# A windowed strain attention with a top-4 of 16 expert layer: the experts' work by dispatch in groups, four strains of eight on TensorE, the damage bias inside its product

## The reference

```
disp = (x @ W_disp)            # 16 heads of 16
strain = disp_win - disp       # 64 earlier positions of each token
bond_act = gelu(strain @ W_strain + rel_emb @ W_pos)
damage_act = gelu(strain @ W_dmg + b_dmg)
damage = sigmoid(damage_act @ W_dmg_out + b_dmg_out)
logits = bond_act @ W_bond - 10.0 * damage
out = softmax(logits) @ val_win @ W_cproj
```

```
vals, idx = top_k(t @ gate_w.T + gate_b, 4); w = softmax(vals)   # 4 of 16 experts per token
h = t @ w1[e] + b1[e];  s = swiglu(h);  y = s @ w2[e] + b2[e]
acc = acc + route[e] * y       # the reference does it for all 16 experts
```

## Time and profile before

| | us |
|---|---|
| median of three runs (range) | 1205.12 (1204.17 to 1207.86) |
| span of the profiled execution | 1203.6 |
| the profiled execution's own time stands among the three runs; its span is below it by | 0.6 to 4.3 |
| set-up block | 0 to 41.1 |
| loop 1, band 1 | 41.1 to 327.5, to 406.0 |
| loop 2, band 2 | 406.0 to 692.5, to 772.0 |
| second layer | 772.0 to 1203.6 |
| busy in the span: PE, DVE, ACT, POOL | 1056.1, 962.4, 821.7, 168.1 |

### The profile page before, as it was taken

One profiled execution on the slowest core, in us unless ns is written; L12 is line 12 of the kernel. 1 busy time (PEld: TensorE's weight loads), 2 busy tenths in 40 slices (PEclk: granted clock), 3 DMA queues, 4 the chain that ended last, 5 costly groups with the idle time before them and its releaser, 6 DMA issues. The chain is left out here.

```text
span 1203.6 us, 23755 instructions
## 1 busy us (share of the span) xinstructions
PE 1056.1 (88%) x9995; PEld 567.0 (47%) x9995; DVE 962.4 (80%) x1193; ACT 821.7 (68%) x888; POOL 168.1 (14%) x265
## 2 busy tenths in 40 slices
PE   6499888998879499889899868999999999999897
PEld 4233333333368333333333368853654565655533
DVE  7899999999763799999999863557778577676757
ACT  3689999999763489999989862243156666665464
POOL 5100000000140100000000050232760000000072
PEclk9699999999979789999999979999779999999899
DMA  8400000000075200000000057000132344523121
GB/s 269 128 2 2 1 1 2 1 1 2 1 204 145 54 1 2 1 1 2 1 1 2 1 172 178 24 1 1 36 105 62 105 132 125 155 80 90 47 60 45
DMA packets 71754, 67.45 MB, mean 56 GB/s; under 512 B 6148, under 2 KB 63200, under 8 KB 71648
## 3 DMA queue, kind: packets, MB, share of 16 engines
q1 hardware_dynamic: 66264, 55.31, 16.1%
q0 software_dynamic: 3840, 10.43, 3.3%
q10 hardware_dynamic: 1544, 0.20, 0.1%
HBM read 41.80 MB, written 20.97 MB: 52 GB/s over the span
## 5 line engine op out<-in xcount | busy, mean ns | idle before, releaser
L580 DVE SCALAR_TENSOR_TENSOR ring<-AD,PT 128x1808 f32<-128x1808 f32 (+15 forms) x128 | 286.1, 2235 | 3.8 <-POOLq L562 1.9
L725 PE MATMUL LG<-ring,lred 128*32 128x456 f32 (+15 forms) x2048 | 233.4, 575 | 2.0 <-ACT ring L677 2.0
L1932 DVE TENSOR_REDUCE MX<-SS 128x2 f32<-128x1024 f32 x119 | 144.6, 1219 | 55.3 <-PE SS L1649 55.2
L1862 ACT ACTIVATE EX<-SS 128x1024 f32<-128x1024 f32 x128 | 130.4, 1031 | 80.4 <-PE SS L1649 79.8
L667 ACT ACTIVATE ring<-ring 128x3616 f32<-128x3616 f32 (+15 forms) x50 | 169.9, 3398 | 3.7 <-DVE ring L580 3.7
L747 PE MATMUL SD<-DS,eyes 96*32 96x456 bf16 (+15 forms) x2496 | 156.2, 369 | 10.1 <-ACT ring L672 8.1
L675 ACT ACTIVATE ring<-ring 128x1824 f32<-128x1824 f32 (+15 forms) x78 | 141.0, 1808 | 0.0
L747 PEld LDWEIGHTS SD<-DS,eyes 96*32 96x32 bf16 x2496 | 58.0, 96 | 154.6 <-ACT ring L672 56.7
L580 DVE SCALAR_TENSOR_TENSOR ring<-AD,bdmg 128x1808 f32<-128x1808 f32 (+15 forms) x50 | 111.4, 2228 | 0.0
L725 PEld LDWEIGHTS LG<-ring,lred 128*32 128x32 f32 x2048 | 59.4, 110 | 100.2 <-issue 76.6
L760 PE MATMUL PY<-w2T,xg 128*128 128x128 f32 x512 | 75.6, 292 | 31.5 <-DVE xg L605 31.5
(11 more groups left out here) (346 smaller groups left out, 1558.0 us busy)
## 6 DMA issues: line engine op xcount, KB each, us to landing
w1s<-in_L_ffn_W SPq DMA_DIRECT2D x39, 256.0 KB, 3.0
w2s<-in_L_ffn_W SPq DMA_DIRECT2D x39, 256.0 KB, 2.9
band<-zs SPq DMA_DIRECT2D x8, 1024.0 KB, 9.9
wide<-band POOLq DMA_DIRECT2D x16, 380.0 KB, 8.3
wide<-band SPq DMA_DIRECT2D x16, 380.0 KB, 10.0
band<-Z SPq DMA_DIRECT2D x4, 1024.0 KB, 7.7
xs<-Z SPq DMA_DIRECT2D x4, 640.0 KB, 8.0
xl<-xs SPq DMA_DIRECT2D x10, 256.0 KB, 2.9
```

The source lines that it names most:

```text
L580: return v.scalar_tensor_tensor(out=ring[:, slot, s, :, t0:T], in0=AD[:, s, :, j + t0:j + T], scalar=extra, in1=AD[:, s, :, PAD + t0:PAD + T],
L725: mm = pe.matmul(LG[32 * b:32 * b + 32, par, s, t0:T], lred[:, s, n % 4, :], ring[:, slot, s, b, t0:T], start=(n % 4 == 0), stop=(n % 4 == 3))
L1862: act.activation(EX[:, Q % 2, hh:hh + 2, t, :], SS[:, slot, :, :], ACT.Exp, scale=SCALE1).then_inc(freed[slot], 1)
L1932: v.tensor_reduce(MX[:, t, p // 2, hh:hh + 2], pairs_of(b, name), AX.X, ALU.max).then_inc(freed[slot], 1)
```

## The change

**Experts by dispatch.** Each token's four slots in a buffer sorted by expert, in tiles of 128 rows, are computed in the first body of loop 1 (`count`, `starts`, `tables` on TensorE, `expert_tiles`, `token_slots`, `tile_tables` on VectorE). POOL scatters the normalised rows into DRAM (`xs0`) with 64 indirect transfers. 80 tiles, in 20 groups of four (A and B of a body), go through bodies 4 to 7 of loop 1 and 0 to 5 of loop 2 (MOE_ITS). For a group, SP loads the rows (`tokens`, one buffer `xl`), four first weights (`weights1`, two buffers) and four second weights (`weights2`, one buffer), each weight's address from a table value that it loads first, and stores the result (`store`). TensorE turns the rows (`turn`), and then the steps are as before, in four pieces of 128 where the expert differs; `move_out` copies the result out. In the end POOL gathers each token's four rows (64 indirect transfers: 32 in loop 2 after the last group, 32 in band 2), and VectorE adds them with `add_rows`.

**Strains.** PE_ITEMS becomes (1, 3, 5, 7), in the first body (3, 5, 7): VectorE makes four damage strains of eight (before, three), TensorE four (before, five), in alternation.

**Bias.** The product takes 99 rows in place of 96: the three parts of `b_dmg` against rows of ones in `DS`, which POOL writes once per loop (3 rows of 9216); the Gelu needs no bias operand.

**Zeroing.** The clearing of `band` and of the second layer's `xs` goes from the set-up block into loop 1 on SP; `xs0` is cleared in the set-up block, and both weight stacks are written to DRAM there.

The core of the diff:

```diff
-PE_ITEMS = (1, 2, 4, 6, 7)
-AFTER_PE = (2, 7)
-FIRST_PE_ITEMS = (2, 4, 6, 7)
+PE_ITEMS = (1, 3, 5, 7)
+FIRST_PE_ITEMS = (3, 5, 7)
 NPE = len(PE_ITEMS)
 LOOP_PE = 7 * NPE + len(FIRST_PE_ITEMS)
...
+MOE_ITS = ((4, 5, 6, 7), (0, 1, 2, 3, 4, 5))
...
+    def gather(pool, k, half, dst):
+
+        for t in range(8 * half, 8 * half + 8):
+            pool.indirect_dma_start(dst[:, t, :], None, ys0[:, :], bass.IndirectOffsetOnAxis(ap=sloti[:, t, k:k + 1], axis=0),
+                                    bounds_check=ROWS0 - 1, oob_is_err=True).then_inc(d_yg[half] if k < 3 else d_yh, 16)
...
+                def tokens(n):
+                    sp.wait_ge(tok_turned, n)
+                    sp.dma_start(xl[:], xs0[4 * P * n:4 * P * n + 4 * P, :].rearrange("(n p) c -> p n c", p=P)).then_inc(d_xl, 16)
+
+                def weights1(n):
+                    if n >= 2:
+                        sp.wait_ge(h_ready, n - 1)
+                    for a in range(4):
+                        e = sp.value_load(owneri[0:1, 4 * n + a:4 * n + a + 1], min_val=0, max_val=E0 - 1)
+                        sp.dma_start(w1s[:, n % 2, a, :], w1d[bass.ds(e, 1), :, :].rearrange("o p i -> p (o i)")).then_inc(d_w1[n % 2], 16)
+
+                def weights2(n):
+                    if n:
+                        sp.wait_ge(y_ready, n)
+                    for a in range(4):
+                        e = sp.value_load(owneri[0:1, 4 * n + a:4 * n + a + 1], min_val=0, max_val=E0 - 1)
+                        sp.dma_start(w2s[:, a, :], w2d[bass.ds(e, 1), :, :].rearrange("o p c -> p (o c)")).then_inc(d_w2, 16)
+
+                def store(n):
+                    sp.wait_ge(y_used, n + 1)
+                    sp.dma_start(ys0[4 * P * n:4 * P * n + 4 * P, :].rearrange("(n p) c -> p n c", p=P), yo[:]).then_inc(d_ys, 16)
...
+                    sp.wait_ge(d_small, 96)
+                    sp.wait_ge(small_pool, 6)
+                weights1(groups[0])
+                weights2(groups[0])
+                if g == 0:
+                    sp.wait_ge(d_scatter, 16 * TT * K0)
+                tokens(groups[0])
+                for n in groups:
+                    if n + 1 in groups:
+                        weights1(n + 1)
+                        tokens(n + 1)
+                        weights2(n + 1)
+                    store(n)
+                sp.wait_ge(d_ys, 16 * (groups[-1] + 1))
...
+                    for t in range(TT):
+                        for k in range(K0):
+                            pool.indirect_dma_start(xs0[:, :], bass.IndirectOffsetOnAxis(ap=sloti[:, t, k:k + 1], axis=0), TF[:, t, :], None,
+                                                    bounds_check=ROWS0 - 1, oob_is_err=True).then_inc(d_scatter, 16)
+                else:
+                    pool.wait_ge(d_ys, 16 * GROUPS0)
+                    for k in range(2):
+                        for half in range(2):
+                            if k:
+                                pool.wait_ge(added, 2 * k + half - 1)
+                            gather(pool, k, half, yg0)
...
+                    A, B_ = moe_groups(g, it)
+                    before = moe_groups(g, it - 1)[1] if it else None
+                    item(4, it)
+                    item(5, it)
+                    move_out(before)
                     if it:
                         logits(1, 2 * it - 1)
...
+                    item(6, it)
+                    glu_in(A)
...
+                    item(7, it)
+                    move_in(B_)
+                    item(8, it)
+                    glu_out(A)
                     logits(0, 2 * it)
-                    glu_out(3, u + 3)
-                    combine(2, it, u + 2)
...
+                        tile_tables()
...
+                    item(9, it)
...
+                        add_rows(v, 0, 1, yg0)
+                    item(10, it)
+                    move_out(A)
+                    item(11, it)
+                    glu_out(B_)
+                    if (g, it) == (1, 7):
+                        add_rows(v, 1, 0, yg0)
...
-                            for q in range(4):
-                                mm = pe.matmul(SD[32 * q:32 * q + 32, i, t0:T], eyes[0:96, sign, :], DS[0:96, q, 2 * half + i, at:at + T - t0],
-                                               start=(sign == 0), stop=(sign == 1))
+                    for i in range(2):
+                        for q in range(4):
+                            pe.matmul(SD[32 * q:32 * q + 32, i, t0:T], eyes[0:99, q, :], DS[0:99, q, 2 * half + i, j + t0:j + T],
...
+                def turn(n):
+                    if n is not None:
+                        pe.wait_ge(d_xl, 16 * (n + 1))
+                        pe.wait_ge(xg_ready, n)
+                        for a in range(4):
+                            mm = pe.transpose(PH[:, P * a:P * a + P], xl[:, a, :], ident[:])
+                        mm.then_inc(tok_turned, 1)
...
+                    A, B_ = moe_groups(g, it)
+                    before = moe_groups(g, it - 1)[1] if it else None
+                    after = moe_groups(g, it + 1)[0] if it < 7 else None
+                    strain(3, it, 0)
+                    reduce(1, it)
+                    expert_out(before)
...
+                    strain(3, it, 1)
+                    reduce(2, it)
+                    hidden(A)
+                    strain(5, it, 0)
+                    reduce(3, it)
+                    turn(B_)
+                    strain(5, it, 1)
+                    reduce(4, it)
...
                     strain(7, it, 0)
...
+                    reduce(5, it)
+                    hidden(B_)
                     strain(7, it, 1)
...
+                    reduce(6, it)
+                    expert_out(A)
+                    strain(9, it, 0)
+                    reduce(7, it)
+                    strain(9, it, 1)
+                    reduce(8, it)
+                    turn(after)
+
+                if g == 0:
+                    count()
+                reduce(0, 0)
+                turn(moe_groups(g, 0)[0])
...
+                else:
+                    for half in range(2):
+                        pool.wait_ge(added, 3 + half)
+                        gather(pool, 2, half, yg0)
+                    read(pool, 0, 1)
+                    gather(pool, 3, 0, yg1)
+                    read(pool, 1, 1)
+                    gather(pool, 3, 1, yg1)
+                    read(pool, 2, 1)
+                    read(pool, 3, 1)
```

More of the change, by code:

```diff
@@ L92, in pe_item, with moe_groups @@
     return LOOP_PE * g + (NPE * it - NPE + len(FIRST_PE_ITEMS) if it else 0) + pe_items(it).index(n)
+def moe_groups(g, it):
+    if it not in MOE_ITS[g]:
+        return None, None
+    first = 2 * (len(MOE_ITS[0]) * g + MOE_ITS[g].index(it))
+    return first, first + 1
 def dram_rows(tensor, offset, dims):
@@ L608, in combine, with expert_tiles @@
[L608 to L621 removed]
+                def expert_tiles():
+                    v.wait_ge(small_pe, 7)
+                    link(v.tensor_tensor(held[:], PYf[0:E0, 0:TT], bound[:], ALU.is_gt))
+                    link(v.tensor_reduce(tiles[:], held[:], AX.X, ALU.add))
+                    v.tensor_scalar(tiles_m[:], ones[0:E0, :], tiles[:, 0:1], float(P), ALU.mult, ALU.mult)
+                    v.tensor_scalar(tiles_n[:], ones[0:E0, 0:NTILE0], tiles[:, 0:1], 1.0, ALU.mult, ALU.mult).then_inc(small_dve, 1)
@@ L653, in _ @@
+                v.tensor_tensor(parts[2], rest, parts[1], ALU.subtract).then_inc(parts_dve, 1)
+                item(1, 0)
+                item(2, 0)
+                if g == 0:
+                    expert_tiles()
                 v.wait_ge(d_parts, 192 * (g + 1))
-                glu_in(0, 0, U0)
+                item(3, 0)
                 for it in range(8):
                     body(it)
+                move_out(moe_groups(g, 7)[1])
                 logits(1, 15)
+                if g:
+                    add_rows(v, 1, 1, yg0)
```

538 lines of the change are left out of this document (331 added, 207 removed).

## The result

The changed kernel takes **1401.37 us** (median of four runs, 1385.28 to 1407.39) against 1204.64 for the kernel before measured beside it: ratio **1.158**, 95% interval 1.152 to 1.165. It is slower, as forecast, but by 197 us, not by 140, and outside the range. That one took 1407.39 with a span of 1405.6, 202.0 more than that of before.

What follows compares the result with a forecast made beforehand. VectorE's list was taken to set the pace, 33.3 us per body. Loop 1 +52, loop 2 +68 and band 2 +19 gave 139 on a span of 1203.6, so 1345 us; range 1275 to 1385.

Steps and rivals of the forecast that it cites:

- a circle over SP's queue: Bodies with two groups: store, weights and rows queue on SP, so 38.4 us, then 42.7 in steady state, not 32.0.
- Loop 2: Second loop: late rows, bodies with two groups, clock loss and the gathers' tail give 354 against 286.5 us, +68.
- The bodies without experts: Four in loop 1, two in loop 2: ScalarE sets 28.7 us, 4.6 less than now.
- Loop 1: First loop: blocked scatter, bodies with two groups and clock loss end it at 380 against 327.5 us, +52.
- Steps with one answer ... nothing: 99 contracted rows, Gelu without bias, swapped clearings, small VectorE steps, POOL's rows of ones: covered, costing nothing.
- The scatter: Loop 1: POOL's 64 indirect transfers blocked by VectorE's strains, one per strain; first turn at 212, 34 us late.
- Band 2: Second band stage: 16 gathers ahead of POOL's first read, turning 17.6 later, VectorE's additions 1 to 2: +19 us.
- The clock: TensorE's slower clock after idling at waits for rows: 1.2 us each, 7 waits in loop 1, 10 in loop 2.
- loads covered: Rival: rows arrive in time, bodies with experts 32.0 to 33.3 us, 1189 if band 2's reads are too; faster: chance 0.05.

Runs made afterwards that it cites:

- the mended kernel: Changed kernel with credit before the rows of ones, two row buffers with SP's new order, glu_in(A) ahead of item 6: 1313.7 us, 1.043 times the kernel before.
- three of four orders: Second band stage's 32 gathers reordered against the changed kernel (stage 109.4 us): the three others, turning sooner, took 110.7, 111.1 and 127.3 us.

## Why the prediction was right or wrong

Right: the direction, and the main mechanism. The loads close a circle over SP's queue, a body with two groups costs 39.6 and then 46 us, not 32, and with a second buffer and SP's order mended 82 us come back, none of them through the buffer alone. Loop 2 was forecast at +68 and measured +74.5. The bodies without experts took 27.0 to 28.3 us (by the starts of ScalarE's `tanh`, 92.46 to 174.70) where 28.7 were forecast. Part of it is the Gelu without its bias, put at nothing: a TensorE item of 928 columns took ScalarE 3.29 us, 3.48 before. Loop 1 gains nothing by it, for it waits for the scatter.

The sum was 63 us short (139 against 202.0 in the spans). The step that carries the result out of the range is the scatter; with it fail the rows of ones and VectorE's additions, both put at next to nothing. By the steps of the sum:

- **"Steps with one answer ... nothing"**: POOL's rows of ones were to be covered because they "must end before the first TensorE strain, some 15 us into the loop". I looked at who uses the rows and not at what is queued behind them on POOL: VectorE's first credit. It cost 8 us (the run with the credit first: 8.1 and 7.8).
- **"The scatter"**: one transfer per strain, first turn at 212. In the pattern in which POOL is let in at each boundary the number held (214.44), in part by luck: without the rows of ones it is 206.10, 6 sooner than forecast, and they made up for it. The step took for granted that a blocked instruction goes in at the end of the one that blocks it; in the profiled execution it was passed over by four to seven strains, five times. It cost 29 us (243.15 against 214.44). The case was not in the range, and this alone carries the result out of it: 1401 - 29 = 1372, below 1385. Why POOL is passed over stays open.
- **"Loop 1", "Loop 2"**: from the first turn to the end of loop 1 168 were forecast and 178.8 came: 4 in the three bodies, 6 in the last, where TensorE also waited 4.05 for second weights (`416.54`). In loop 2 the first turn was 3.6 earlier, the bodies 4.6 and the end 6 longer.
- **"Band 2"**: the first turning was forecast 17.6 later and was 18.7 later. But the later steps stretch from 53.3 to 63.6 us, where "VectorE's additions cost 1 to 2". That term was too small: TensorE waits 4.15 us in two goes for a copy that stands behind them, and about 6 more go with the slow products behind that wait and behind the first turning's (granted clock 0.50 to 0.60, see the rows above), a cost that the prediction charged in the loops and not here. TensorE's stop for "issue" is no part of it: 2.3 us, and 2.9 in the run without gathers.
- **"The clock"**: 1.2 per wait, where the run that fills most of the waits gives 0.8 as the least. Both lie between the prediction's 0 and 2.3; a better value wasn't measured.
- Set-up, band 1 and the second layer: -2.5, -0.5 and +4.5 for nothing forecast.

The first turn is 31 us late: 29 for the passing over and 8 for the rows of ones, less the 6 by which the forecast was high. With the 10.8 behind it, 6.5, 10 and the small ones the 63 are accounted for. The rival "loads covered" named its condition rightly (SP reaches the rows in time), and its bodies of 32.0 to 33.3 came true in the mended kernel; its end on the other side did not, because the scatter still delays loop 1 (first turn at 206 instead of 178) and the band stage keeps its 29 us.

## What to carry to other kernels

Before a clearing or table is costed at nothing, read what is queued behind it on its own engine, a semaphore hand-out above all. Where loads depend on data, write SP's queue in the order in which things are needed and not by group: a second buffer without that order gave nothing here. And indirect transfers can cost more than their own issue time: they can wait far longer than one VectorE instruction, and in three of four orders TensorE stood without instructions beside them, so that moving them about in a stage full of small matmuls gained nothing here. Last, an addition of 2 us put between two copies for which TensorE waits costs its length and, behind it, products at the lower clock.

## What the hardware did that I had not expected

- **POOL passed over.** Beside back-to-back strains of 2.1 us with two SBUF inputs, POOL's instructions either go in at each boundary (1.4 to 2.6 us each) or wait 8.7 to 15.9 us. The two patterns appear with the same program: of the fifteen profiles with the dispatch here eight had the owner table at 14.6 to 14.7 us, one had only later transfers at 10 to 15, and six were free in loop 1. The Trainium skill (SBUF — State Buffer, Who interferes with whom) has the blocked one wait for the other's whole instruction; a wait over four to seven of them is beyond that. It also infers that descriptor generation needs the write interface. The transfers here were held all the same; they also read their indices from SBUF, so this doesn't tell which of the two was blocked.
- **TensorE short of instructions.** While POOL issues one gather per 1.31 us, TensorE can run dry: 50 products in 35 us at a DMA share of 0.18, and 200 in 28 us at 0.67 to 1.07. It began 9, 20 and 33 us after the stage's first gather in the three orders that turn sooner. In the order of the change it didn't come, though nine of the gathers went out beside TensorE's first turning and the products behind it. That the refill of its instructions is held up behind the gathers is my reading (no instruction packet in the 35 us); what holds it was not tested. The Trainium skill (Runtime: NRT & Kernel Launch, Instruction fetch mechanics) calls the cost of crossing into the next block of instructions mostly hidden; if my reading holds, here it is not.
